# Exchanging k's halves by engine copies in place of DMAs, in an adaLN-style attention and FFN kernel

## The reference

```
q, k, v = proj(x, Wq), proj(x, Wk), proj(x, Wv)
q = q * min(cond, 4)                       # one factor per batch
scores = where(causal, q @ k.T / sqrt(64), min)
a = (softmax(scores) @ v) @ Wo.T
out = x + absmax_int8(a) @ ternary(Wf).T + bias
```

## Time and profile before

| | |
|---|---|
| median of 3 runs | 2062.44 us (2061.98 to 2063.0) |
| the profiled execution: its own time, its span | 2064.0 us, 2062.2 us |
| busy in the span: PE, PEld, DVE, ACT, POOL | 1957.3, 1703.8, 1358.2, 1024.0, 910.6 us |
| attention, 385 to 1585 us: PE, DVE, ACT, POOL busy | 1140.15, 904.29, 845.51, 576.10 us |
| attention: granted clock, DMA share, GB/s | 0.98, 0.73, 254 |

### The profile page before, as it was taken

How to read it: one execution, slowest core, us unless ns; L and a number is a source line. 1 busy time by engine, 2 the same in 40 slices (tenths; PEclk the granted TensorE clock), 3 DMA queues, 4 the chain that set the end, 5 groups by cost and what they waited for, 6 DMA issues and landing times.

```text
span 2062.2 us, 40307 instructions
## 1 busy us (share of the span) xinstructions
PE 1957.3 (95%) x12378; PEld 1703.8 (83%) x12378; DVE 1358.2 (66%) x3330; ACT 1024.0 (50%) x2495; POOL 910.6 (44%) x985
## 2 busy tenths in 40 slices
PE   8999878899998999999999998999988999999998
PEld 6788667899998999998899998999986777777775
DVE  6545665477778777788677777777777645545454
ACT  4443332477776676777677776777675000000000
POOL 1333443344446444455444455444444544444442
PEclk9999999899999999999999999999999999999999
DMA  6899998877777677776777777777772433332322
GB/s 214 323 375 346 358 334 312 290 258 253 253 277 257 239 280 259 269 242 249 277 254 260 260 249 256 258 253 279 259 239 80 141 111 102 103 111 97 117 92 81
DMA packets 165696, 477.83 MB, mean 232 GB/s; under 512 B 12768, under 2 KB 84448, under 8 KB 135776
## 3 DMA queue, kind: packets, MB, share of 16 engines
q1 hardware_dynamic: 165072, 476.11, 66.0%
q10 hardware_dynamic: 528, 0.52, 0.1%
HBM read 331.88 MB, written 111.15 MB: 215 GB/s over the span
## 4 chain that ended last, share of the span: by engine, by line
PE 74%; DMA 9%; DVE 8%; issue 4%; ACT 3%; SPq 1%; POOL 1%; DVEq 0%; ACTq 0%; POOLq 0%
PE proj_ps L211 22%; PE s_ps L596 9%; PE proj_ps L596 8%; DMA parts<-x_scratch 7%; PE t_ps L1010 6%; PE o_ps L375 6%; PE t_ps L337 6%; PE o_ps L667 5%; PE o_ps L1010 4%; PE s_ps L297 3%; PE s_ps L298 3%; DMA xv_raw<-xT 2%; DVE pt_all L361 2%; DVE q_st L274 1%; DVE prob L309 1%
## 5 line engine op out<-in xcount | busy, mean ns | idle before, releaser
L211 PE MATMUL proj_ps<-parts 128*128 128x256 f32 x5376 | 773.9, 292 | 28.4 <-DMA parts<-x_scratch 25.5
L211 PEld LDWEIGHTS proj_ps<-parts 128*128 128x128 f32 x5376 | 681.3, 193 | 42.2 <-issue 19.8
L327 POOL TENSOR_TENSOR prob<-prob,row_inv 128x128 f32<-128x128 f32 (+3 forms) x512 | 375.5, 734 | 612.5 <-DVE row_inv L321 610.6
L315 ACT ACTIVATE prob<-prob,row_min 128x128 f32<-128x128 f32 (+3 forms) x512 | 287.3, 561 | 179.1 <-DVE row_min L309 173.7
L361 DVE TENSOR_TENSOR pt_all<-t_ps,pt_all 128x128 fp32r<-128x128 f32 (+3 forms) x512 | 249.5, 487 | 109.4 <-ACT pt_all L354 108.8
L309 DVE CUSTOM_DVE_ANT_0 prob<-s_ps,mask 128x128 f32<-128x128 f32 (+3 forms) x512 | 247.5, 483 | 35.6 <-PE s_ps L298 11.0
L337 PE MATMUL t_ps<-ident,prob 128*128 128x128 f32 x1280 | 230.5, 278 | 21.0 <-DVE pt_all L361 17.5
L652 ACT ACTIVATE yt_q<-t_ps 128x1024 bf16<-128x1024 bf16 x32 | 32.7, 1023 | 426.7 <-PE t_ps L645 426.7
L354 ACT ACTIVATE pt_all<-t_ps 128x128 fp32r<-128x128 f32 (+3 forms) x512 | 216.8, 423 | 12.3 <-PE t_ps L337 10.6
L337 PEld LDWEIGHTS t_ps<-ident,prob 128*128 128x128 f32 x1280 | 151.0, 141 | 49.0 <-issue 24.8
L297 PE MATMUL s_ps<-k_sw,q_st 128*128 128x128 f32 (+3 forms) x512 | 170.4, 333 | 19.4 <-DVE row_min L309 15.9
(11 more groups left out here) (126 smaller groups left out, 2822.8 us busy)
## 6 DMA issues: line engine op xcount, KB each, us to landing
parts<-x_scratch SPq DMA_DIRECT2D x224, 1024.0 KB, 7.6
x_scratch<-xv SPq DMA_DIRECT2D x112, 512.0 KB, 5.9
k_sw<-k_st SPq DMA_DIRECT2D x128, 256.0 KB, 3.7
xv_raw<-xT SPq DMA_DIRECT2D x17, 1024.0 KB, 8.8
v_scratch<-v_tmp SPq DMA_DIRECT2D x64, 256.0 KB, 5.1
v_raw<-v_scratch SPq DMA_DIRECT2D x32, 512.0 KB, 4.0
oT_scratch<-o_sum SPq DMA_DIRECT2D x64, 256.0 KB, 3.3
o_raw<-oT_scratch SPq DMA_DIRECT2D x32, 512.0 KB, 4.7
```

The costliest lines, as they stand in the source:

```text
L211: mm = pe.matmul(qk_bank(w, m), wc[w][:, c, wp, k, :], xq[:, c, :, xp, k, :], start=(fresh and k == 0 and i == 0), stop=(k == CH - 1 and i ...
L315: act.activation(prob[u % QT], prob[u % QT], ACT.Exp, bias=row_min[:, u % 4:u % 4 + 1], scale=-1.0, accum_out=row_sum[:, u % 4:u % 4 + 1]) ...
L327: pool.tensor_tensor(prob[u % QT], prob[u % QT], row_inv[:, u % 4:u % 4 + 1].broadcast_to([P, w]), ALU.mult).then_inc(norm_done, 1)
```

## The change

The two DMAs for each block go. Their place is taken by one copy on ACT (partitions 64 to 127 of k to partitions 0 to 63 of `k_sw`) and one on POOL (the other half), each of 64 partitions x 1024 elements. POOL's copy is a multiplication by a broadcast 1. Block 0's copies stand at the very end of ACT's and POOL's step lists: on ACT behind q's high part of block 0, so directly ahead of the next step's `H(10)`, on POOL behind `N(12)`. Block 1's stand on ACT behind `H(2)`, on POOL behind `N(4)`. POOL also waits for instructions of its own: ahead of the copy for v's split and for the normalisation before it, behind it for the copy. `S(0)` and `S(8)` wait for both copies. SP's list keeps its order, without the swaps, and ACT's k evacuation no longer waits for the DMAs of the iteration before.

```diff
-            else:
-                if due(count := it * 32):
-                    act.wait_ge(k_swapped[blk], count)
...
-        def swap_k(sp, it, blk):
-            sp.wait_ge(proj_lo_done, it * NEV + EVAC[K, blk])
+        def swap_k(eng, it, blk, part):
             heads = slice(2 * blk, 2 * blk + 2)
-            sp.dma_start(k_sw[0:DH, heads, :].bitcast(F32), k_st[DH:P, heads, :].bitcast(F32)).then_inc(k_swapped[blk], 16)
-            sp.dma_start(k_sw[DH:P, heads, :].bitcast(F32), k_st[0:DH, heads, :].bitcast(F32)).then_inc(k_swapped[blk], 16)
+            dst, src = ((slice(0, DH), slice(DH, P)), (slice(DH, P), slice(0, DH)))[part]
+            eng.wait_ge(proj_lo_done, it * NEV + EVAC[K, blk])
+            if eng is nc.scalar:
+                eng.activation(k_sw[dst, heads, :], k_st[src, heads, :].bitcast(F32), ACT.Copy).then_inc(k_swap_done[part], 1)
+            else:
+                eng.tensor_tensor(k_sw[dst, heads, :], k_st[src, heads, :].bitcast(F32),
+                                  one[src, 0:1].rearrange("p (a b) -> p a b", b=1).broadcast_to([DH, 2, S]),
+                                  ALU.mult).then_inc(k_swap_done[part], 1)
...
             if u % (2 * QT) == 0:
-                pe.wait_ge(k_swapped[h // 2], (it + 1) * 32)
+                for done in k_swap_done:
+                    pe.wait_ge(done, it * NBLK + h // 2 + 1)
...
             H(2)                       # act_step
+            if old:
+                swap_k(act, old[0], 1, 0)
             copy(now, K, COPY_C21)
...
             evacuate(now, Q, 0)        # the last of act_step
+            if now:
+                swap_k(act, now[0], 0, 0)
...
             N(4)                       # pool_step
+            if old:
+                ...
+                pool.wait_ge(v_lo_done, old[0] * HG + 4)
+                pool.wait_ge(norm_done, old[0] * UNITS + 5)
+                swap_k(pool, old[0], 1, 1)
+                pool.wait_ge(k_swap_done[1], old[0] * NBLK + 2)
...
             N(12)                      # pool_step
+            if now:
+                pool.wait_ge(v_lo_done, now[0] * HG + 2)
+                if old:
+                    pool.wait_ge(norm_done, old[0] * UNITS + 13)
+                swap_k(pool, now[0], 0, 1)
+                pool.wait_ge(k_swap_done[1], now[0] * NBLK + 1)
...
-            if old:                    # sp_step, ahead of store_o and load_v
-                swap_k(sp, old[0], 1)
...
-            if now:                    # sp_step, behind load_xq(M_P6)
-                swap_k(sp, now[0], 0)
```

More of the change, by code:

```diff
@@ L150, in adaln_ffn_kernel @@
         proj_lo_done = sem("proj_lo_done")
-        k_swapped = [sem(f"k_swapped{i}") for i in range(NBLK)]
+        k_swap_done = [sem(f"k_swap_{n}_done") for n in ("low", "high")]
         v_in = sem("v_in")
@@ L1695, in pool_step @@
             N(4)
+            if old:
+                if qk_for is not None:
+                    pool.wait_ge(qk_sum_done, 4 * 2 * qk_for + 2)
+                if late_for is not None:
+                    pool.wait_ge(qk_sum_done, 4 * (2 * late_for + 1) + 2)
+                if not now:
+                    pool.wait_ge(wo_lo_done["POOL"], 2)
+                pool.wait_ge(v_lo_done, old[0] * HG + 4)
+                pool.wait_ge(norm_done, old[0] * UNITS + 5)
+                swap_k(pool, old[0], 1, 1)
+                pool.wait_ge(k_swap_done[1], old[0] * NBLK + 2)
             WO(6)
```

## The result

The changed kernel takes 2139.38 us (median of 4 runs, 2138.07 to 2142.28) against 2062.21 us before: a ratio of 1.0378, 95% interval 1.036 to 1.0396. The forecast was slower, 2127 us, with a range from 2075 to 2165. The profiled execution spans 2136.3 us.

What follows compares the result with a forecast made beforehand. The prediction took TensorE, with 74% of the chain, as the bound. It summed 2064.0 + 33 (block 0) + 50 (block 1) - 18 (freed DMA list) = 2129, put at 2127 us because the runs' median lies 1.6 lower; range 2075 to 2165.

Steps and rivals of the forecast that it cites:

- The gain: Taking 128 DMA issues off SyncE's list saves 16 us of waits for x and 2 at the first S(0): 18 us.
- allowed for in one stretch only: The half-clock stretch at 696.6 follows a wait for x and may itself go: 1.6 us, within the range.
- Block 1's place: GpSimd's copy behind N(4) meets VectorE's low parts of q; TensorE stands 1.55 us a step, 32 times: 50 us.
- The rule read from the earlier trace: In two collisions, VectorE's instruction with two SBUF inputs was held and ended 0.55 us after GpSimd's.
- The prediction's 6 us for that rule: Taking the skill's shared-port rule word for word would add 0.2 us at each collision, 6 us in all.
- the forecast's case with VectorE first: In block 1, VectorE's first low part ends at 512.5, GpSimd's copy about 514.25, the second part at 514.8: 1.5 us late.
- The seam: Where loop steps meet, block 0's copies delay H(10), L(10), low parts of q and S(0): 1.07 us, 31 times, 33 us.
- either copy alone would cost about the same: For block 0, were ScalarE's copy free, GpSimd's would cost about the same 1 us; 1.07 taken for both.
- At the changes of group the lists of GpSimd and VectorE are fuller, and I take the same: Steps at changes of group were charged the same as loop steps: 1.07 us for block 0, 1.55 for block 1.
- the free port: GpSimd's copy does not hold VectorE, so only ScalarE's 1.04 us a step is paid: 2076 us; chance 0.12.
- copies in idle time: Block 0's copies fit into idle time where steps meet, block 1's ScalarE copy into its 1.10 us: 2044 us; chance 0.08.
- The clock's rival: Stalls may bring 3.2 us stretches at half clock, 1.6 us each; one in each of 31 steps gives 2177 us; chance 0.15.

Runs made afterwards that it cites:

- without an exchange: Kernel before with neither DMAs nor copies for exchanging k, the scores using k unexchanged: 2044.00 us, ratio 0.9927.
- seam alone: Changed kernel with only block 0's two copies kept, block 1's scores using k twice: 2082.48 us, ratio 1.0093.
- block 1 alone: Changed kernel with only block 1's two copies kept, block 0's scores using k twice: 2102.62 us, ratio 1.0192.
- the loads first: Kernel before with two loads of x put ahead of block 0's DMA exchange on SyncE's list, no engine copies: 2106.47 us, ratio 1.0188.
- the last version: Changed kernel with all copies moved, GpSimd's a one-input copy, and the fourth split of v left ahead of N(4): 2053.53 us, ratio 0.9962.

## Why the prediction was right

*The gain* was put at 18 us, at the first `S(0)` and at x; measured 15 (ratio) to 18 (stretch). The size was right, what it is made of only in part. The wait at the first `S(0)` is gone, and lies ahead of that stretch. In the traces 14.1 of the 18.1 us lie in four steps at the changes of group. In the kernel before, these four hold 17.1 us at half clock, and without an exchange none. Three other steps there lost 6.0 us of waits for x and became only 0.9 us shorter. At 1.6 us for 3.4 us at half clock, as in the run with ScalarE's copy moved, some 8 us of the gain are the clock, which the prediction had allowed for in one stretch only. That the sum of the waits came out is so far luck.

*Block 1's place*: the mechanism and the size in the loop were right. VectorE began first, the copy ran on, and the pair of low parts came out 1.52 us late (forecast 1.5); the loop step with block 1's copies alone is 1.55 longer (forecast 1.55). The rule read from the earlier trace rows, that the held instruction ends 0.55 us after GpSimd's, came out at 0.54 to 0.55, in all 58 such meetings of the changed kernel. The Trainium skill, page "SBUF — State Buffer", section "SBUF: two separate sides", would have the loser wait until the other has ended and then run in full, 0.76 us here; the trace keeps to 0.54. (The prediction's 6 us for that rule are 0.2 us once a step; with its two meetings a step they would be 13.) GpSimd's own instruction was lengthened as well, from 1.89 to 2.35 us, as the forecast's case with VectorE first has it: there the copy ends 1.75 us behind the first low part, and it did, though the prediction shows no row for that figure. Where it shows was wrong: not the transposition, as I had said, but `S(8)` takes the wait first, 1.15 us.

*The seam*: 1.24 us in place of 1.07. ScalarE's copy delays `H(10)` and `L(10)` by 1.09, and the low parts still catch the tail of GpSimd's copy, 0.11 (1.64 in place of 1.53). That either copy alone would cost about the same was right at full clock, by the runs that move one of them. Where it shows was wrong: I had named `S(0)` with 1.4 us, but `T(12)` needs the late `L(10)` first and takes 0.89 of it.

*The step that was mis-sized* is "At the changes of group the lists of GpSimd and VectorE are fuller, and I take the same", and with it the clock, which the sum leaves at full speed. From the first to the last `S(0)` the changed kernel is 92.7 us longer than the one without an exchange (1228.3 to 1135.6). The 22 steps outside the changes of group make 57.7 of them (2.75 in each of 20, 0.4 in the first, 2.3 in the last), where 22 x 2.62 gives 57.6. The nine at the changes make 35.0 in place of 23.6, so 3.89 a step and not 2.62. These 11.4 us are most of what the forecast fell short by (2139.4 - 2127 = 12.4). The nine steps hold 20.5 us at half clock, and without an exchange none. At 1.6 us for 3.4 us that is some 9 to 10 of the 11.4, an estimate. So the stalls themselves were about as long as in the loop, though in the step shown above (2.96 - 1.39 = 1.57) by another way, the order of GpSimd's list and not the port. What was missing is the clock behind them. In the loop steps it stayed at full speed, as forecast.

For the whole change by these stretches: -18.1 (gain) + 38.5 (seam alone) + 60.5 (block 1 alone) = +80.9, and measured +74.6 (1228.3 - 1153.7). Of the 6.3 us by which both together cost less than each alone, 2.9 lie in the first two steps and the last, 1.7 at the changes of group, where the slow stretches fall differently, and the rest is about 0.1 in each ordinary step.

The rivals: the free port fell (the pair took 3.05 us), and copies in idle time fell as placed (they are reached by the last version, at other places and with a shorter copy). The clock's rival was met in the changed kernel at the changes of group only; in loop steps it was met with ScalarE's copy moved and with the loads first.

## What to carry to other kernels

An operation moved to an engine with idle time costs what stands right behind it in that engine's list, and on a shared port what another engine starts meanwhile: here the change cost 77 us with the copies at one set of places and 8 with the same copies at another; with a shorter copy on GpSimd and one split left in its place it gave 8. Before placing one, go through the next two or three instructions on that engine and see who waits for them, in the ordinary step and in each special one. And sum a stall by the longer step, not by the waits that the profile names: part of those were there before.

## What the runs showed of the hardware that was not expected

- A stall of TensorE in one piece of 1.55 us was followed by 3.4 us at half clock in 12 of 19 loop steps; pieces of 0.89 and 0.46 us, in loop steps as long at full clock, were not, in any of them. That the pieces are the reason was not tested by itself. The Trainium skill, page "TensorE: Matmul & The Clock Gate", section "HAM oscillation — how this bites in real kernels", has a repeated wait, there 3 to 5 us long, lower the clock each time. With these shorter stalls the first kernel agrees with it in part, the second not in its loop steps.
- GpSimd copies 64 x 1024 in 1.03 us with one input and in 1.89 by a multiplication with a broadcast 1. Where a low part of q on VectorE had begun first, they took 1.28 to 1.41 and 2.23 to 2.35 us. Both hold the low part that meets them until 0.54 to 0.55 us after their own end.
- Two 1 MB loads ahead of an exchange of two DMAs of 256 KB on the same list made TensorE's scores wait for it 20 times, 42.3 us, where before there was one wait of 2.9 us that names no releaser.
